# Attention scores from the parts of q and k in row tiles of 32, instead of stacked copies of them

## What is computed

```python
h = jnp.maximum(_layernorm(x, axis=-1), 0.0)
x = x + _L0_gnn_ref(h, adj, adj, L0_gnn_b)      # max over features of relu(adj @ h + b), per node
h = jnp.maximum(_layernorm(x, axis=-1), 0.0)
x = x + _L1_gnn_ref(h, w_qkv, w_proj, b_proj, ln_gamma, ln_beta, adj)

# _L1_gnn_ref: 8 heads of 32 features
qkv = (x @ w_qkv).reshape(b, n, 3, H, hd).transpose(2, 0, 3, 1, 4)
attn = jnp.einsum('bhnd,bhmd->bhnm', q, k) * scale
attn = jnp.where(attn_mask[None, None] == 0, -jnp.inf, attn)
attn = jax.nn.softmax(attn, axis=-1)
o = jnp.einsum('bhnm,bhmd->bhnd', attn, v)
o = o @ w_proj + b_proj
return o + layernorm(o)
```

## Time and profile before

| | before |
|---|---|
| median of 3 runs | 840.02 us (835.99 to 840.54) |
| the profiled execution | 831.87 us |
| its span, first to last instruction | 830.1 us |
| TensorE busy | 748.7 us, 90% |
| VectorE busy | 602.5 us, 73% |
| ScalarE busy | 496.8 us, 60% |
| GpSimd busy | 386.7 us, 47% |
| mean granted TensorE clock | 0.979 |

### The profile page before, as it was taken

The page is one execution under the profiler, slowest core; times in us unless marked ns, Lnnn a source line. Parts: engine busy times, 40 slices in busy tenths (PEclk is TensorE's granted clock), DMA queues, the critical chain, the costliest instruction groups (busy, mean ns, idle before and its releaser), DMA issues.

```text
span 830.1 us, 28573 instructions
## 1 busy us (share of the span) xinstructions
PE 748.7 (90%) x11113; PEld 501.6 (60%) x11113; DVE 602.5 (73%) x1488; ACT 496.8 (60%) x1160; POOL 386.7 (47%) x720
## 2 busy tenths in 40 slices
PE   1768999999999999999999999999999999999661
PEld 0335666666666666666666666666666666666441
DVE  2545778877787778877777778777777887777643
ACT  3535766766666657666566666665666676655440
POOL 3612455445554554455544554544545444543343
PEclk9989999999999999999999999999999999999986
DMA  7557686768766887867777877888678787654322
GB/s 199 119 152 147 143 173 155 166 141 169 151 151 160 169 165 155 171 145 146 156 161 172 174 158 158 151 164 139 155 163 162 163 166 142 146 104 110 57 42 30
DMA packets 167325, 121.39 MB, mean 146 GB/s; under 512 B 83732, under 2 KB 166420, under 8 KB 166676
## 3 DMA queue, kind: packets, MB, share of 16 engines
q1 hardware_dynamic: 67336, 69.75, 32.6%
q10 hardware_dynamic: 82960, 33.04, 22.0%
q0 software_dynamic: 16896, 16.78, 14.9%
HBM read 35.06 MB, written 33.55 MB: 83 GB/s over the span
## 4 chain that ended last, share of the span: by engine, by line
PE 57%; DVE 14%; SPq 10%; issue 9%; DMA 5%; ACT 3%; ACTq 1%; POOL 1%; DVEq 0%; POOLq 0%
PE a_ps L315 13%; SPq L263 10%; DVE smax L680 10%; PE a_ps L328 8%; PE pv_ps L408 7%; PE sc_ps L388 6%; PE sum_ps L411 5%; PE sc_ps L337 5%; PE sum_ps L438 4%; PE sc_ps L360 4%; DMA stack<-pairs 3%; PE a_ps L298 2%; PE pv_ps L423 1%; DVE st L713 1%; ACTq L525 1%
## 5 line engine op out<-in xcount | busy, mean ns | idle before, releaser
L680 DVE TENSOR_REDUCE smax<-sc_ps 128x4 f32<-128x512 f32 x256 | 164.2, 684 | 24.7 <-PE sc_ps L360 22.8
L672 DVE TENSOR_TENSOR pairs<-a_ps,pairs 128x512 f16<-128x512 f32 x128 | 87.2, 683 | 118.4 <-ACT pairs L561 118.2
L571 ACT ACTIVATE p_sb<-sc_ps 128x512 f32<-128x512 f32 x256 | 146.1, 602 | 44.6 <-PE sum_ps L411 33.7
L845 POOL TENSOR_TENSOR h_parts<-h_sb,h_parts 128x256 f16<-128x256 f32 x128 | 84.3, 670 | 133.7 <-ACT h_parts L518 133.4
L315 PE MATMUL a_ps<-hT,w_hi 128*128 128x512 f16 x512 | 134.1, 384 | 11.6 <-DVE mask_n L785 11.6
L851 POOL TENSOR_TENSOR oT_lo<-oT,oT_hi 128x256 f16<-128x256 f32 x128 | 85.6, 669 | 106.3 <-ACT oT_hi L584 106.3
L561 ACT ACTIVATE pairs<-a_ps 128x512 f16<-128x512 f32 x128 | 76.0, 596 | 91.8 <-issue 52.8
L408 PE MATMUL pv_ps<-p_sb,v_sb 128*32 128x128 f32 x2048 | 107.6, 278 | 15.4 <-ACT pv_sb L578 9.2
L879 POOL DMA_DIRECT2D out<-y_sb x32 | 43.1, 1348 | 159.5 <-DVE y_sb L735 159.5
L411 PE MATMUL sum_ps<-p_sb,sel_sum 128*32 128x128 f32 x2048 | 105.6, 273 | 0.0
L360 PE MATMUL sc_ps<-stack 96*128 96x128 f16 x1024 | 83.7, 222 | 9.6 <-DMA stack<-pairs 9.6
(11 more groups left out here) (92 smaller groups left out, 1395.5 us busy)
## 6 DMA issues: line engine op xcount, KB each, us to landing
stack<-pairs SPq DMA_DIRECT2D x768, 64.0 KB, 3.0
out<-in_x SPq DMA_DIRECT2D x32, 512.0 KB, 4.2
out<-y_sb POOLq DMA_DIRECT2D x32, 512.0 KB, 6.5
x_sb<-in_x ACTq DMA_DIRECT2D x31, 512.0 KB, 6.1
stack<-crow SPq DMA_DIRECT2D x64, 8.0 KB, 4.4
w_sb<-in_L_gnn_w_qkv SPq DMA_DIRECT2D x1, 768.0 KB, 5.3
hT<-h_parts ACTq DMA_TRANSPOSE x33, 6.2
x_sb<-in_x SPq DMA_DIRECT2D x1, 512.0 KB, 4.2
```

What stands on the lines that cost most here:

```text
L571: nc.scalar.activation(p_sb[:, u % P_SLOTS], sc_ps[u % SC_SLOTS][:], ACT.Exp, scale=SCALE).then_inc(p_ready, 1)
L672: nc.vector.tensor_tensor(pairs[:, 1 - c % 2, c // 2, c % 2], a_ps[c % 2][:], pairs[:, c % 2, c // 2, c % 2], ALU.subtract).then_inc(qklo_ ...
L680: nc.vector.tensor_reduce(smax[:, HC * j:HC * (j + 1), b], sc_ps[u % SC_SLOTS][:], AX.X, ALU.max).then_inc(smax_ready, 1)
L845: nc.gpsimd.tensor_tensor(h_parts[:, par, 1, b], h_sb[:, b], h_parts[:, par, 0, b], ALU.subtract).then_inc(hlo_ready, 1)
```

## The change

- `stack`, `pairs`, `stack_heads`, `max_rows` and `ms_row` go. `qk_high` and `qk_low` write into `qk_hi` and `qk_lo`, with two slots each.
- `scores` and `scores_T` take a head's 32 partitions straight from these: per batch, three products of the parts for each of four heads, each head in its own strip of 32 rows and its own bank `sc_ps[i]`. A bank now holds one head for four batches, where it held four heads of one batch. `scores_T` adds a fourth product that brings in the maxima.
- `smax` is laid out on 128 columns and repeated (`repeat_max`), so that one full transpose puts the maxima on all 128 partitions; `max_high` and `max_low` write high and low parts on alternate rows of `crow`, and `ms_sel` selects the unit's rows. There is no DMA in it.
- Three stages in place of four: scores of group t in step t, the rest of attention of group t-1 in step t, PV of the last four units and the output in step t of group t-2. There are 34 steps.
- PV is made in two runs of four units (P0 to P3, then Y0 to Y3 in the next step), and `take_pv`, `spread`, `scale_o` and `o_high` work on two batches at once.
- `transpose_h` and `load_x` go from ScalarE's queue to SyncE's. All orders are rewritten, and constants are built earlier.

The core of the diff:

```diff
-            def stack_heads(t, slot, j):
...
-                for i in range(HC):
-                    head = slice(HD * i, HD * (i + 1))
...
-                    for blk, src in enumerate((high, pairs[head, 0, j], pairs[head, 1, j])):
-                        dst = stack[blk * HD:(blk + 1) * HD, slot, :, HC * j + i]
-                        nc.sync.dma_start(dst.rearrange("p s b n -> p s (b n)"), src).then_inc(stacked[j], 16)
-            ORDER = ("C0 Q0 M0 Q1").split()
+            ORDER = ("C0 T0 X0").split()
...
+            def scores(t, j):
+
+                pe.wait_ge(qkhi_ready, 4 * t + 2 * j + 2)
+                pe.wait_ge(qklo_ready, 4 * t + 2 * j + 2)
+                for b in range(G):
+                    for q, k in ((qk_hi, qk_hi), (qk_lo, qk_hi), (qk_hi, qk_lo)):
+                        for i in range(HC):
+                            head = slice(HD * i, HD * (i + 1))
+                            mm = nc.tensor.matmul(sc_ps[i][:, b], q[head, t % 2, j, 0, b], k[head, t % 2, j, 1, b],
+                                                  start=False, stop=True, skip_group_check=True)
+                mm.then_inc(s_psum, 1)
+
+            def transpose_max(t):
+                pe.wait_ge(smax_twice, t + 1)
+                nc.tensor.transpose(sc_ps[0][:, 0, :], smax[:].rearrange("p i s j b -> p (i s j b)"),
+                                    identf[:]).then_inc(maxT_psum, 1)
+
+            def mask_scores_T(g, j, a):
                 if j == 0:
+                    pe.wait_ge(clo_ready, g + 1)
+                elif a:
+                    pe.wait_ge(smax_ready, UNITS * (g + 1) + HC)
...
+            def scores_T(g, j):
+
+                for b in range(G):
+                    for k, q in ((qk_hi, qk_hi), (qk_hi, qk_lo), (qk_lo, qk_hi)):
+                        for i in range(HC):
+                            head = slice(HD * i, HD * (i + 1))
+                            nc.tensor.matmul(sc_ps[i][:, b], k[head, g % 2, j, 1, b], q[head, g % 2, j, 0, b],
+                                             start=False, stop=True, skip_group_check=True)
+                    for i in range(HC):
+                        head = slice(HD * i, HD * (i + 1))
+                        mm = nc.tensor.matmul(sc_ps[i][:, b], ms_sel[head, G * j + b], crow[head],
+                                              start=False, stop=True, skip_group_check=True)
+                mm.then_inc(st_psum, 1)
...
+                if u == 0:
+                    pe.wait_ge(p_ready, UNITS * (g + 1))
...
-            ORDER = ("K0 S0 S1 R0 S2 Q0 S3 R1 Q1 N0 E0 R2 O0 E1 E2 E3 L0 O1 R3 K1 S4 S5 O2 S6 S7 L1 O3 N1 M0 E4 "
-                     "E5 E6 P0 P1 Q2 P2 P3 Q3 P4 P5 E7 V0 P6 P7 V1").split()
+            ORDER = ("Q0 Y0 Y1 Y2 Y3 N0 E0 Q1 R0 Q2 K0 S0 R1 O0 Q3 O1 L0 N1 E1 O2 L1 O3 K1 S1 V0 V1 P0 P1 P2 P3 M0").split()
...
             def exps(g, u):
+                j, i = u // HC, u % HC
+                act.wait_ge(st_psum, DC * g + j + 1)
+                if u == 0:
+                    wait(act, pv_psum, UNITS * g)
+                nc.scalar.activation(p_sb[:, j, i], sc_ps[i][:], ACT.Exp, scale=SCALE).then_inc(p_ready, 1)
...
+            ORDER = ("Y0 Q0 E0 E1 E2 Q1 E3 C0 Q2 R0 R1 R2 O0 C1 R3 H0 Q3 H1 H2 H3 O1 E4 E5 O2 E6 E7 O3 V0 L0 A0 M0 V1").split()
...
+            def row_max(t, u):
+                j, i = u // HC, u % HC
+                dve.wait_ge(s_psum, DC * t + j + 1)
...
+            def repeat_max(t):
+                dve.wait_ge(smax_ready, UNITS * (t + 1))
+                nc.vector.tensor_copy(smax[:, :, 1], smax[:, :, 0]).then_inc(smax_twice, 1)
+
+            def max_low(t):
+                dve.wait_ge(chi_ready, t + 1)
+                wait(dve, st_psum, DC * t)
...
+            ORDER = ("I0 I1 Q0 I2 O0 Q1 Q2 O1 S0 S1 S2 S3 Q3 B0 X0 B1 B2 L0 B3 L1 G0 S4 S5 S6 S7 F0 U0 F1 F2 F3 X1 M0").split()
...
+                if t == 0:
+                    row_constants()
...
+            def row_constants():
+                dve.wait_ge(pool_const, 6)
...
+            ORDER = ("C0 C1 C2 C3 H0 H1 H2 H3 N0 W0 W1 W2 K0 W3 D0 X0").split()
...
             invert_std_x(1, 1)
+            later_constants()
             pipeline(step)
```

More of the change, by code:

```diff
@@ L265, in _, with load_x @@
-            ORDER = ("C0 Q0 M0 Q1").split()
-            def step(t, k, a, sc, e, d, prep, norm, load):
-                if t == 2:
-                    sp.wait_ge(ms_rows, 1)
-                    for slot in range(1, SLOTS):
-                        nc.sync.dma_start(stack[STACK:ROWS, slot, 1].rearrange("p h b n -> p (h b n)"),
-                                          stack[STACK:ROWS, 0, 1].rearrange("p h b n -> p (h b n)")).then_inc(ms_copied, 16)
+            def load_x(t, par):
+                wait(sp, h_ready, G * (t - 2))
+                sp.wait_ge(x_loaded, 16 * t)
+                nc.sync.dma_start(x_sb[:, par], xg[t]).then_inc(x_loaded, 16)
@@ L273, in step @@
+            ORDER = ("C0 T0 X0").split()
+            def step(t, k, a, e, d, prep, norm, load):
                 for what in ORDER:
@@ L276, in step @@
                         copy_x(t)
-                    elif kind == "Q" and a:
-                        stack_heads(t, k, i)
-                    elif kind == "M" and sc:
-                        max_rows(t - 1, (k + 2) % SLOTS)
+                    elif kind == "T" and prep:
+                        transpose_h(t + 1, (k + 1) % SLOTS)
+                    elif kind == "X" and load:
+                        load_x(t + 3, k)
+            load_x(1, 1)
+            first_transposes()
+            load_x(2, 2)
             pipeline(step)
@@ L350, in mask_scores @@
-                put_mask(mask_q)
-            def scores(g, par, u):
-                j, b = u // G, u % G
-                if b == 0:
-                    pe.wait_ge(stacked[j], 16 * DMAS * (g + 1))
-                to = sc_ps[u % SC_SLOTS]
-                for i in range(HC):
-                    h = HC * j + i
-                    mm = nc.tensor.matmul(to[:, i], stack[0:STACK, par, 0, h, b], stack[0:STACK, par, 1, h, b],
-                                          start=False, stop=True, skip_group_check=True)
-                mm.then_inc(s_psum, 1)
@@ L382, in scores_T, with values @@
+            def values(g, par, u):
                 b, j = u // DC, u % DC
+                if u % PAIR == 0:
+                    pe.wait_ge(v_ready, 2 * g + b // 2 + 1)
+                    wait(pe, pv_ready, 2 * g + b // 2)
                 if u == 0:
-                    pe.wait_ge(crow_in, 32 * (g + 1))
-                to = sc_ps[u % SC_SLOTS]
-                for i in range(HC):
-                    h = HC * j + i
-                    mm = nc.tensor.matmul(to[:, i], stack[0:ROWS, par, 1, h, b], stack[0:ROWS, par, 0, h, b],
-                                          start=False, stop=True, skip_group_check=True)
@@ L390, in scores_T @@
[L390 to L401 removed]
+                    pe.wait_ge(p_ready, UNITS * (g + 1))
+                    wait(pe, oT_ready, 2 * g)
@@ L580, in o_high, with max_high @@
-            def o_high(g, b):
-                act.wait_ge(oT_ready, G * g + b + 1)
-                if b == 0:
+                if c == 0:
+                    wait(act, st_psum, DC * (t - 1))
+                nc.scalar.activation(qk_hi[:, t % 2, c // 2, c % 2].rearrange("p b n -> p (b n)"), a_ps[c % 2][:],
+                                     ACT.Copy).then_inc(qkhi_ready, 1)
+            def max_high(t):
+                act.wait_ge(maxT_psum, t + 1)
+                wait(act, clo_ready, t)
+                nc.scalar.activation(cpart[:], sc_ps[0][:, 0, :], ACT.Copy, scale=max_flag[:, 0:1]).then_inc(chi_ready, 1)
@@ L611, in step @@
                         take_v(t, k, i)
-                    elif kind == "M" and sc:
-                        max_high(t - 1)
+                    elif kind == "M" and a:
+                        max_high(t)
                     elif kind == "E" and e:
-                        exps(t - 2, i)
+                        exps(t - 1, i)
                     elif kind == "A" and e:
-                        take_pv(t - 2, i)
+                        take_pv(t - 1, 0)
+                    elif kind == "Y" and d:
+                        take_pv(t - 2, 1)
                     elif kind == "O" and d:
-                        take_o(t - 3, i)
+                        take_o(t - 2, i)
                     elif kind == "C" and d:
-                        o_high(t - 3, i)
-                    elif kind == "X" and load:
-                        load_x(t + 3, k)
+                        o_high(t - 2, i)
                     elif kind == "R" and prep:
```

337 lines of the change are left out of this document (138 added, 199 removed).

## The result

The changed kernel takes 778.45 us, median of four runs (777.61 to 781.43); the kernel before took 839.52 on the same chip (835.99 to 840.54). The ratio is 0.9308, 95% interval 0.928 to 0.9336: 6.9% faster. The forecast was 786, 7.5 us above the measurement, where the whole gain is 61. The profiled execution took 781.43 us, its span is 779.7 against 830.1.

A forecast was written before the change was run, and what follows sets the result against it. TensorE's work was taken to bound the kernel. Start 36, second step 21.2, 30 steps of 22.35 and tail 48 gave a span of 775.7; plus 1.8 and the 8.1 run offset, forecast 786 us, range 774 to 826.

The forecast's parts named there:

- What binds: Whole span: TensorE's list of work bounds the kernel, busy 90% of the span before, with 57% of the chain.
- Groups of four: Scores: 56 groups of four side-by-side 32-row matmuls at 0.057 us replace 64 full-array matmuls, minus 0.39 us a step.
- Changes of shape: TensorE's switches between tile shapes: 11 a step at 0.10 us, 1.1 us against 1.2 before.
- `o_sb` ahead of O3: Output projection in a regular step: TensorE waits 0.20 us for o_sb.
- The wait of K1: Regular step: TensorE waits 0.13 us for the last exp.
- the rival in which hT or a handoff takes the place of the old wait: Regular step: late row maxima and exps, or hT's longest landing, cost one us more a step, 818 us; chance 0.12.
- The step: Regular step's length: laid out at 22.2 us, taken as 22.25, or 22.35 with unevenness, against 23.17 before.
- The 0.10 of unevenness: Added to each regular step for late steps that remain once the stack and row DMAs go: 0.10 us.
- The ends: Start and tail: first transpose of maxima at 36 us, the second 21.2 later, 48.2 from last transpose to end.
- The sum: Span: 36 + 21.2 + 30 x 22.35 + 48 = 775.7 us, against 830.1 before.
- The step that was mis-sized most: From profiled time to median of runs: the offset of 8.1 us seen before, making 777.5 into 785.7.
- The lower end of the range: Whole time: down to 774 us, with run offset 4, groups at 0.056 us and no unevenness.

The follow-up runs named there:

- e2: Changed kernel with every score matmul streaming 64 of its 128 columns, all instructions kept: 749.79 us, ratio 0.9011.
- e1: Changed kernel with the score matmuls reordered, one strip's three products written one after another before the next strip's: 782.06 us, ratio 0.9399.
- e5: Changed kernel with PV's run of four split by half of project_v, two more tile-shape changes a step: 786.60 us, ratio 0.9412.
- e7: Changed kernel with PV directly behind the scores and project_v last, ScalarE taking V later and building its constants in step 0: 783.08 us, ratio 0.9378.
- e4: Kernel before with stacks filled for the first three groups only, later groups reusing them, every matmul kept: 823.31 us against 835.62, ratio 0.9854.
- e12: Against e7: four of PE's waits dropped in the program so a step has 1024 instructions, 96 small matmuls added at the start: 772.62 us, ratio 0.9235.

## Why the prediction was right, and where its numbers were off

**What binds.** Right: PE is 90% of the chain, and no DMA, no "issue" of ScalarE and no stack holds PE in a regular step.

**Groups of four.** Predicted 0.057, 48 matmuls in 0.68 and 64 in 0.91; measured 0.056, 0.69 and 0.90. The row that I put next to it, the mask's burst, was the right one to choose; the 27 ns a pair of PV were no limit (7.4 ns in `e2`). One idea beside it, written down for `e1`, was wrong: that the order of the matmuls was needed.

**Changes of shape.** Taken at 0.10; 0.12 by the two that `e5` adds, 0.10 and 0.11 by starts, and 0.15 for the one that `e7` removes together with its change of ScalarE's order. 11 of them at 0.12 are 0.2 us a step more than the sum had.

**Waits.** `o_sb` ahead of O3 was laid out at 0.20. In PE's timeline of after, between layer 0 and the next output projection:

```profile
409.94 0.38 PE L291 MATMUL a_ps<-h_parts,adjT_lo 128*128 128x512 f16 x1
410.36 0.27 PE L424 MATMUL sum_ps<-bp_rows,bias_ones 128*128 128x256 f16 x1
```

0.42 from start to start, of which a matmul of 512 columns streams 0.215: 0.20, as said. The wait of K1 was 0.04 for 0.13. hT landed after 4.3 to 6.6 us, median 4.7, where I kept 6.2. The stacks' DMAs were the reason: in `e4`, the kernel before without them, the median is 4.3. So the rival in which hT or a handoff takes the place of the old wait lost its ground.

**The step.** Laid out 22.2, taken 22.25 and 22.35 with unevenness; the regular step was 22.32, the mean of the 30 steps in the sum 22.47 in the first profile and 22.33 in the second. The 0.10 of unevenness was taken for queues; what came in its place was in part PE's supply of instructions, which I had not thought of. That the term came near is luck.

**The ends.** The first transpose at 34.41 for 36: the constants that VectorE's `row_constants` waits for were there at 22.2 and the first `qk_low` started at 22.6, where I had 23.8 and 24.5. The next 20.96 later, for 21.2. The tail was 50.21 for 48.2. I had carried over 4.1 us of slower clock, but this tail has a mean granted clock of 0.73 (before 0.80), and two rows of it show the lower level, 1.2 GHz: groups 0.107 apart behind PE's waits for `oT_hi` and `o_sb`.

```profile
737.17 0.27 PE L424 MATMUL sum_ps<-bp_rows,bias_ones 128*128 128x256 f16 x1 [1.44 <-ACT oT_hi L555]
...
740.84 0.32 PE L375 MATMUL sc_ps<-qk_lo,qk_hi 32*128 32x128 f16 x4
740.95 0.32 PE L375 MATMUL sc_ps<-qk_hi,qk_lo 32*128 32x128 f16 x4
```

**The sum.** The span was to be 775.7 (the last term taken as 48) and was 779.7. By terms: start -1.6, second step -0.2, 30 steps +3.6, tail +2.2.

**The step that was mis-sized most is the last one.** I added 8.1 us for how far the profiled execution of before lay under the median of its runs, as if that belonged to the kernel. In every execution of after in these runs the time stands some 2 us over the span; the rest is spread between executions. Before's median was 831.18 to 839.52 from one set of runs to the next, and the profiled one happened to be low. After's profiled execution lay 3.0 above its median. So this term is 11.1 us too high and the span 4.0 too low, and the forecast lies 7 us over the measurement. Without the 8.1 the sum would have been 777.5, 1 us off, and that would have been luck too: the span's 4.0 and the 3.0 by which the profiled execution stood over the median go against each other. The lower end of the range, 774, doesn't follow from its own three terms either: 775.7 + 1.8 + 4, less 3.0 for the unevenness and 1.7 for the groups, is 776.8.

## What to carry to other kernels

A stacked contraction over 3 x 32 rows can be had as three products in four row strips at the same price on TensorE, 0.056 us for a group of four at 128 columns in any order, and it frees the queues of the copies that the stack needs. When matmuls become many and short, count TensorE's instructions: the standstills here came behind blocks of 256 that ran in 3.1 to 6.0 us, mostly beside DMA traffic. A loop body that is a multiple of 256 long keeps the borders in one place; where that place is good it helps in every step, as in `e12`, and a bad one would cost in every step, which no run tried. And judge a reordering by its regular step as well as by its time: `e7` was the better order and the slower kernel, until the borders were moved.

## What was not expected of the hardware

- Matmuls in different row strips overtake each other: a strip's three products, written one after another, were started four strips at a time (0.69 us for 48 in either order).
- Four row strips take new weights every 0.030 us at 64 columns, 7.4 ns for a load and its matmul.
- TensorE stood still for 0.17 to 2.4 us, 52 times in 1,579 blocks, at one place of its blocks of 256 instructions: wherever the next block's packet landed less than 1.21 us before it was due, and nowhere where it landed more than 1.27 us before.
